# A decoder layer on one core: operand splits around the end of the latents, two products alternating, a longer last stretch by rows

## The chip, the cores and the metric

The kernel runs on one core of one Trainium2 chip, whose other cores have nothing to do. The metric is the time of one execution on the device in microseconds (us); lower is better. The kernel before takes 638.35 us, the median of 3 runs (637.8 to 639.55).

## What is computed

The layer has an attention, a second product with a context after quantization, and a feed-forward part with a routed branch, each followed by a residual and a normalization. The change lies in the feed-forward part alone, on `[2, 512, 1024]` tokens:

```python
logits = jnp.einsum('bsh,he->bse', hidden_states, gate_w)
routing_weights, selected_experts = jax.lax.top_k(logits, K)
h = jax.nn.relu(jnp.einsum('bsh,hi->bsi', hidden_states, up_w)) ** 2
shared_out = jnp.einsum('bsi,ih->bsh', h, down_w)
x_latent = jnp.einsum('bsh,hl->bsl', hidden_states, fc1_w)
expert_out = jnp.einsum('bsl,lm->bsm', x_latent, expert_w)
moe_out = expert_out * jnp.sum(routing_weights, axis=-1, keepdims=True)
routed_out = jnp.einsum('bsl,lh->bsh', moe_out, fc2_w)
return _layernorm(shared_out + routed_out, ln_gamma, ln_beta)
...
x = _layernorm(x + _L0_ffn_ref(x, ...), axis=-1)
```

K is 2, INT (hidden) 2048, LAT 512. Everything is float32 of full precision, so every product on TensorE is three: each operand is split into a high part (what the array's format holds) and a low part (the rest), and hi·hi, hi·lo and lo·hi are added in PSUM (`split_products`).

## The kernel before, in words

`decoder` runs `attention_and_cross` (the first 209 us) and then, behind a barrier of all engines, `feed_forward`. That is written by hand: one program for each engine, in the order in which its instructions stand, held together by semaphores. `then_inc` on an instruction counts its semaphore up, and `wait_ge` holds all that stands behind it on that engine.

**Products up.** `MU` = 20 blocks m of 128 hidden or latent rows, 8 contraction tiles k each, for batches 0 and 1: `product(m, b)` is 24 matmuls of 128x512 (8 tiles, three products) into one of four PSUM banks `acc_b`. The stationary operand is the weight block, whose parts `u_hi` (ScalarE) and `u_lo` (VectorE) are made by a `split_u(m)` on each of the two; the moving operand is the token matrix, transposed. Batch 0's is there when the feed-forward begins, and so are the products (0, 0) and (1, 0). Batch 1's is made at the beginning: `transpose_x1(k)` is four transposes of TensorE into a bank of `acc_a`, `x1T_hi_out(k)` on ScalarE copies it, `x1T_lo_out(k)` on VectorE subtracts, and `product(0, 1)` takes tile k as it comes, with `transpose_x1(k + 2)` behind it (two banks). Then come four small transposes of the routing logits (`transpose_logits(0)`), and `product(1, 1)`. On VectorE, `route(0)` stands behind the eight `x1T_lo_out`: it reads the transposed logits, and turns them into the routing weights; behind it stand `split_u(2)` and `split_u(3)`. GpSimd adds beta to the rows of the residual meanwhile (`add_beta`, L2030). Blocks 16 to 19 of the up products are the latents: VectorE multiplies them by the routing weights (`latent(m, b)`).

**Products down.** The second matrix product is done by a scheme with seven products instead of eight (`PHASES`, in the order p1, p7, p6, p4, p5, p2, p3). Each phase has NP = 10 contraction tiles k for BT = 4 row tiles t; a step (k, t) is three matmuls of 128x512, a pair of k's (`j`) is 24. The left operand of a pair is split into `oa` (three slots, `oa_hi_out` on ScalarE, the low part by `lo_out` on VectorE); the right one into `ob` (`ob_hi_out`, and `lo_out` again), except in p2 and p3, where it lies split in DRAM and is loaded by GpSimd's queue (`load_split`, 1 MB a pair, once the slot's last reader is done). Each phase fills four PSUM banks, `acc_a` and `acc_b` in turn. On VectorE the last thing before the phases is `latent(19, 1)`, which waits for the very last up product; `lo_out("p1", 0)` stands behind it.

**The end.** p3 runs k outermost for its first tiles, and for its last `TAIL` = 6 tiles row by row, so that rows t = 0 to 3 are complete one after the other. For each, VectorE adds (`p3_out`), takes statistics, centres, scales and adds the residual (`half_stats`, `centre`, `add_x2`); ScalarE squares and takes roots (`first_root`, `last_root`) and normalizes (`final_norm`); SyncE's queue stores the row tile, 512 KB.

Of the kernel before, what the change touches and what calls it, by code (L numbers as in the profile page):

```python
# [17 lines left out]
F32 = mybir.dt.float32  # L18
# [1244 lines left out]
NX = 4  # L1263
TAIL = 6
PHASES = ("p1", "p7", "p6", "p4", "p5", "p2", "p3")
# [13 lines left out]
def step(phase, j):  # L1279
    return PHASES.index(phase) * PAIRS + j  # L1280


def feed_forward(nc, so, args, x2_dram, w2_dram, t_dram, r_dram, x2b_dram, out):
# [8 lines left out]
    with ExitStack() as ctx:  # L1292
# [8 lines left out]
        xT_hi, xT_lo = [so["x2T_hi"], x1_hi], [so["x2T_lo"], x1_lo]  # L1301
        f1b0, f2b0, f1b1 = [sb(n, [P, NP, SEQ], F32) for n in ("f1b0", "f2b0", "f1b1")]
# [10 lines left out]
        pairs_of = lambda x, i: x[:, 4 * i:4 * i + 4].rearrange("p (s h) c -> p s h c", h=2)  # L1313
        oa = [pairs_of(x, i) for x, i in ((xT_hi[0], 0), (xT_hi[0], 1), (xT_lo[0], 0))]
        ob = [pairs_of(x, i) for x, i in ((xT_lo[0], 1), (x1_hi, 0), (x1_hi, 1), (d_op, 0), (d_op, 1))]
# [20 lines left out]
        stage_hi, stage_lo = [[x[h][:, KH // 2:NP] for x in stage] for h in range(2)]  # L1336
        acc_b, acc_a = [so["psum"][:, i:i + BT] for i in (0, BT)]
        acc_of = lambda phase: (acc_a, acc_b)[PHASES.index(phase) % 2]

# [11 lines left out]
            b_hi_done b_lo_done eps_done beta_done st_done mv_done rootA_done rsA_done gam_done res_done nmean_done square_done  # L1351
            rootB_done rsB_done nb_done out_done""".split()
        S = {**so["sem"], **{n: sem("f_" + n) for n in names}}
# [14 lines left out]

        order = [b * BT + t for b in (1, 0) for t in range(BT)]
        half_of = lambda b, t, n: ffn[b * BT + t][:, n * BANK:(n + 1) * BANK]  # L1370
        up_products = BATCH * 2 * UP
# [21 lines left out]
        def a_raw(phase, j):  # L1393
            return s3_of(j) if phase == "p7" else pair({"p1": f1b0, "p6": f1b0, "p5": f1b1, "p4": f2b1, "p3": f1b0, "p2": f2b0}[phase], j)

        def ob_slot(s):
# [23 lines left out]
        def _(sp):  # L1420
# [69 lines left out]
            for n in range(BT, TILES):  # L1490
                load_x2(n)
            for n in range(TILES):
                i = order[n]
                sp.wait_ge(S["out_done"], n + 1)
                sp.dma_start(out_rows[i * P:(i + 1) * P, :], ffn[i]).then_inc(out_st, 16)
            sp.wait_ge(out_st, 16 * TILES)

        @block.tensor
        def _(pe):
            def transpose_x1(k):  # L1500

                if k >= 2:
                    pe.wait_ge(S["x1T_lo_done"], k - 1)
                for t in range(BT):
                    mm = pe.transpose(acc_a[:, k % 2, t * P:(t + 1) * P], x2_tok[:, t, k * P:(k + 1) * P], ident[:])  # L1505
                mm.then_inc(S["x1T_ready"], 1)
# [19 lines left out]
            def spread_r(b):  # L1526
# [5 lines left out]
                mm.then_inc(S["rT_ready"], 1)  # L1532

            def product(m, b):

                q = product_index(m, b)
                if q >= 4 and q - 4 < up_products:
                    pe.wait_ge(S["relu_done"], q - 3)
                elif q >= 4:
                    pe.wait_ge(S["lat_done"], q - 4 - up_products + 1)  # L1540
                pe.wait_ge(S["u_lo_done"], m + 1)
                for k in range(KT):
                    if b and m == 0:
                        pe.wait_ge(S["x1T_lo_done"], k + 1)
                    st = [u[:, m % 2, k] for u in (u_hi, u_lo)]
                    for i, (s, v) in enumerate(split_products(st, (xT_hi[b][:, k], xT_lo[b][:, k]))):
                        mm = pe.matmul(acc_b[:, q % 4], s, v, start=(k == 0 and i == 0), stop=(k == KT - 1 and i == 2))  # L1547
                    if (m, b) == (0, 1) and k + 2 < KT:
                        transpose_x1(k + 2)
                mm.then_inc(S["op_used"], 1)  # L1550

            def tile_step(phase, k, t):
# [18 lines left out]
                if t == 0 and k % 2 == 0:  # L1571
# [3 lines left out]
                    else:  # L1575
                        pe.wait_ge(ob_in[ob_slot(s)], 16 * ((s - PARKED) // PAIRS + 1))
                st = [oa[s % RD][:, k % 2, i, t * P:(t + 1) * P] for i in range(2)]
                for i, (a, v) in enumerate(split_products(st, [ob[ob_slot(s)][:, k % 2, i] for i in range(2)])):
# [34 lines left out]
        def _(act):  # L1613
            def x1T_hi_out(k):
                act.wait_ge(S["x1T_ready"], k + 1)
                act.activation(x1_hi[:, k], acc_a[:, k % 2], ACT.Copy).then_inc(S["x1T_hi_done"], 1)  # L1616

# [30 lines left out]
            def oa_hi_out(phase, j):  # L1648
                s = step(phase, j)
                if s >= RD:  # L1650
                    consumed(act, s - RD)
                else:
                    act.wait_ge(S["op_used"], product_index(MU - 1, 0) + 1)
                a_ready(act, phase, j)
                act.activation(oa[s % RD][:, :, 0], a_raw(phase, j), ACT.Copy).then_inc(S["oa_hi_done"], 1)  # L1655

# [28 lines left out]
            def final_norm(n):  # L1685
                i = order[n]
                act.wait_ge(S["nb_done"], n + 1)
                act.activation(ffn[i], ffn[i], ACT.Identity, bias=nbias[:, n:n + 1], scale=rstd[:, 1, n:n + 1]).then_inc(S["out_done"], 1)

# [54 lines left out]
            first_root(1)  # L1744
            oa_hi_out("p3", 0)
            final_norm(0)
            last_root(1)
            first_root(2)
            oa_hi_out("p3", 1)
            final_norm(1)  # L1750
            last_root(2)
            first_root(3)
            oa_hi_out("p3", 2)
            final_norm(2)
            last_root(3)
            oa_hi_out("p3", 3)
            final_norm(3)
            oa_hi_out("p3", 4)
            first_root(BT)
            for n in range(BT, TILES):  # L1760
                last_root(n)
                if n + 1 < TILES:
                    first_root(n + 1)
                final_norm(n)

        @block.vector
        def _(dve):
            def x1T_lo_out(k):
                dve.wait_ge(S["x1T_hi_done"], k + 1)
                dve.tensor_tensor(x1_lo[:, k], acc_a[:, k % 2], x1_hi[:, k].bitcast(F32), ALU.subtract).then_inc(S["x1T_lo_done"], 1)  # L1770

# [74 lines left out]
            def lo_out(phase, j):  # L1846
                s = step(phase, j)
                dve.wait_ge(S["oa_hi_done"], s + 1)
                dve.tensor_tensor(oa[s % RD][:, :, 1], a_raw(phase, j), oa[s % RD][:, :, 0].bitcast(F32), ALU.subtract).then_inc(S["oa_lo_done"], 1)
# [145 lines left out]
            last_bias(0)  # L1995
            add_x2(1)
            centre(2, 2 * BT)
            lo_out("p3", 0)
            last_bias(1)
            add_x2(2)  # L2000
            centre(3, 2 * BT)
            lo_out("p3", 1)
            last_bias(2)
            add_x2(3)
            lo_out("p3", 2)
            p2_out()
            last_bias(3)
            lo_out("p3", 3)
            for n in range(BT, TILES):
                half_stats(n, 0)  # L2010
            lo_out("p3", 4)
            for t in range(BT):
# [6 lines left out]
                add_x2(n)  # L2019
            last_bias(TILES - 1)  # L2020

        @block.gpsimd
# [118 lines left out]
```

## Time and profile before

| | |
|---|---|
| median of 3 runs | 638.35 us (637.8 to 639.55) |
| the profiled execution | 643.53 us, its span 641.7 us |
| outside the span | 1.83 us |
| mean granted clock of TensorE | 0.979 |
| busy: TensorE, VectorE, ScalarE, GpSimd | 93%, 59%, 47%, 19% of the span |
| chain that ended last | TensorE 62%, VectorE 4%, ScalarE 1% |
| largest lines of it | L1547 (up products) 32%, L1579 (phases) 28% |

The span is from the first to the last instruction. The chain is followed back from the last instruction, at each step to what released it. Times in the rows below are from the span's start. The granted clock is 1.00 at 2.4 GHz and 0.50 at 1.2 GHz.

### The profile page before, as it was taken

How to read it: one execution, taken by the hardware profiler on the slowest of the kernel's cores; microseconds unless marked ns; L12 is line 12 of the kernel's file. 1: busy time of each engine (PE TensorE's matmuls, PEld its weight loads, DVE VectorE, ACT ScalarE, POOL GpSimd, SP SyncE). 2: the span in 40 equal slices, each digit the busy share in tenths (PEclk: the TensorE clock that was granted, in tenths of full speed). 3: DMA queues.
4: the chain of work that ended last, by engine and by line, in shares of the span. 5: the costliest groups of instructions: out<-in, count | busy, mean ns of one | idle time of the engine just before them, and what ended most of it. 6: DMA issues, size and time to landing. Idle time of an engine off the chain costs nothing.

```text
span 641.7 us, 9374 instructions
## 1 busy us (share of the span) xinstructions
PE 597.9 (93%) x3718; PEld 480.2 (75%) x3728; DVE 379.6 (59%) x514; ACT 299.4 (47%) x384; POOL 121.3 (19%) x162
## 2 busy tenths in 40 slices
PE   2799999898999799999999999998999999999991
PEld 1687877566776588788888888877888888888881
DVE  4937898889663373335333331419764565749875
ACT  4456687896693534333333331022344333314625
POOL 2811254635441042222110000000000000021000
PEclk9899999999999899999999999997999999999997
DMA  9766675583663868699799664003333336089903
GB/s 335 273 175 179 189 198 157 156 271 100 192 199 131 295 215 309 219 332 361 231 362 307 253 229 164 0 1 107 94 97 97 98 99 230 1 281 323 279 36 131
DMA packets 82108, 123.61 MB, mean 193 GB/s; under 512 B 23824, under 2 KB 50704, under 8 KB 82064
## 3 DMA queue, kind: packets, MB, share of 16 engines
q1 hardware_dynamic: 74592, 95.21, 44.4%
q0 software_dynamic: 5168, 19.40, 9.6%
q10 hardware_dynamic: 2304, 8.39, 4.0%
q8 instruction: 30, 0.49, 0.3%
q14 instruction: 14, 0.11, 0.1%
HBM read 83.13 MB, written 35.65 MB: 185 GB/s over the span
## 4 chain that ended last, share of the span: by engine, by line
PE 62%; DVE 4%; ACT 1%; issue 0%; DVEq 0%; ACTq 0%
PE psum L1547 32%; PE psum L1579 28%; PE psum L1505 0%; DVE stat_n L1901 0%; DVE x1T_lo L1770 0%; DVE ffn_lo L1920 0%; DVE ffn_hi L1920 0%; DVE ffn_hi L1909 0%; DVE ffn_lo L1909 0%; ACT x1T_hi L1616 0%; PE psum L1513 0%; PE psum L1514 0%; PE psum L1531 0%; DVE ffn_hi L1894 0%; ACT hx L1679 0%
## 5 line engine op out<-in xcount | busy, mean ns | idle before, releaser
L1774 DVE TENSOR_TENSOR u_lo<-u_raw,u_hi 128x1024 fp32r<-128x1024 f32 x18 | 23.8, 1320 | 84.3 <-ACT u_hi L1621 84.3
L1547 PE MATMUL psum<-x1T_hi,u_hi 128*128 128x512 f32 x160 | 63.4, 396 | 2.4 <-DVE x1T_lo L1770 2.4
L1547 PE MATMUL psum<-x1T_hi,u_lo 128*128 128x512 f32 x160 | 62.8, 392 | 0.0
L1547 PE MATMUL psum<-x1T_lo,u_hi 128*128 128x512 f32 x160 | 62.7, 392 | 0.0
L1579 PE MATMUL psum<-x2T_lo,x2T_hi 128*128 128x512 f32 x240 | 58.9, 403 | 3.1 <-DVE x2T_lo L1852 3.1
L1579 PE MATMUL psum<-x1T_hi,x2T_hi 128*128 128x512 f32 x264 | 61.5, 389 | 0.0
L1579 PEld LDWEIGHTS psum<-x1T_hi,x2T_hi 128*128 128x128 f32 x264 | 49.6, 188 | 10.3
L1579 PEld LDWEIGHTS psum<-x2T_lo,x2T_hi 128*128 128x128 f32 x240 | 47.0, 196 | 13.6 <-issue 3.5
L1547 PE MATMUL psum<-x2T_hi,u_hi 128*128 128x512 f32 x144 | 56.3, 391 | 0.0
L1547 PE MATMUL psum<-x2T_lo,u_hi 128*128 128x512 f32 x144 | 56.1, 389 | 0.0
L1547 PE MATMUL psum<-x2T_hi,u_lo 128*128 128x512 f32 x144 | 56.0, 389 | 0.0
L2046 POOL DMA_DIRECT2D x1T_hi<-r_scratch x4 | 2.8, 711 | 251.8 <-PE psum L1579 251.8
L1579 PE MATMUL psum<-x1T_hi,x2T_lo 128*128 128x512 f32 x216 | 50.4, 389 | 0.0
L341 PE MATMUL psum<-w_hi,xT_hi 128*128 128x512 f32 (+1 forms) x128 | 35.9, 363 | 13.7 <-POOL w_lo L1132 8.2
L1579 PEld LDWEIGHTS psum<-x1T_hi,x2T_lo 128*128 128x128 f32 x216 | 40.6, 188 | 8.4
L1655 ACT ACTIVATE x2T_hi<-f1b 128x1024 fp32r<-128x1024 f32 x14 | 14.8, 1060 | 53.3 <-PE psum L1579 38.1
L1547 PEld LDWEIGHTS psum<-x1T_hi,u_hi 128*128 128x128 f32 x160 | 30.2, 189 | 9.5 <-DVE x1T_lo L1770 2.2
L1547 PEld LDWEIGHTS psum<-x1T_hi,u_lo 128*128 128x128 f32 x160 | 30.3, 189 | 6.2
L1547 PEld LDWEIGHTS psum<-x1T_lo,u_hi 128*128 128x128 f32 x160 | 30.2, 189 | 5.9
L341 PE MATMUL psum<-w_lo,xT_hi 128*128 128x512 f32 (+1 forms) x128 | 34.5, 352 | 0.0
L341 PEld LDWEIGHTS psum<-w_hi,xT_hi 128*128 128x128 f32 x128 | 20.5, 196 | 18.6 <-issue 8.8
L341 PE MATMUL psum<-w_hi,xT_lo 128*128 128x512 f32 (+1 forms) x128 | 34.2, 349 | 0.0
(255 smaller groups left out, 1220.2 us busy)
## 6 DMA issues: line engine op xcount, KB each, us to landing
d_raw<-in_L_ffn_down_w_dram SPq DMA_DIRECT2D x20, 512.0 KB, 7.2
t_scratch<-d_raw SPq DMA_DIRECT2D x20, 512.0 KB, 5.8
d_raw<-t_scratch SPq DMA_DIRECT2D x20, 512.0 KB, 3.8
c_sb<-in_ctx_dram ACTq DMA_DIRECT2D x16, 512.0 KB, 3.6
u_raw<-in_L_ffn_up_w_dram SPq DMA_DIRECT2D x16, 512.0 KB, 5.2
r_scratch<-f1b SPq DMA_DIRECT2D x10, 512.0 KB, 5.3
r_scratch<-f2b SPq DMA_DIRECT2D x10, 512.0 KB, 4.6
x_sb<-in_x_dram SPq DMA_DIRECT2D x8, 512.0 KB, 5.2
```

Of the source, the lines that this page charges most:

```text
L341: mm = pe.matmul(qkv_ps[:, c0:c1], s, v, start=(k == 0 and i == 0), stop=(k == KT - 1 and i == 2))
L1547: mm = pe.matmul(acc_b[:, q % 4], s, v, start=(k == 0 and i == 0), stop=(k == KT - 1 and i == 2))
L1579: mm = pe.matmul(acc_of(phase)[:, t], a, v, start=(k == 0 and i == 0), stop=(k == NP - 1 and i == 2))
L1655: act.activation(oa[s % RD][:, :, 0], a_raw(phase, j), ACT.Copy).then_inc(S["oa_hi_done"], 1)
L1774: dve.tensor_tensor(u_lo[:, m % 2], u_raw[:, m % 2], u_hi[:, m % 2].bitcast(F32), ALU.subtract).then_inc(S["u_lo_done"], 1)
L2046: pool.dma_start(ob[ob_slot(s)].rearrange("p s h c -> p s (h c)"), r_dram[k * P:(k + 2) * P, n].rearrange("(s p) h c -> p s (h c)", p=P)). ...
```

## The change

Four edits, all in `feed_forward`:

1. **Batch 1 of blocks 0 and 1.** `first_products` takes the place of `product(0, 1)`, `transpose_logits(0)`, `product(1, 1)`. Three banks of `acc_a` (0, 1 and 3) hold transposed tiles, so three groups of transposes stand at the head. For k = 0 to 2 tile k of block 0 is followed by tile k of block 1; block 1's tiles 3 to 7 stand behind all of block 0's. `transpose_logits(0)`, which uses bank 3, stands behind both.
2. **Low parts between the last latents.** On VectorE `lo_out("p1", 0)` stands between `latent(19, 0)` and `latent(19, 1)`.
3. **`TAIL` = 8.** p3's left operand gets two more slots (`oa_last`, in the memory of `f2b0`, free once p2's operand is split), and pairs 0 and 1 of p3 are written without waiting for p2's pairs to be used; `lo_out("p3", ...)`, `oa_hi_out("p3", ...)`, `last_bias(3)` and `p2_out()` change places with it.
4. **The last row tile.** VectorE normalizes its first 512 columns and ScalarE the others; SyncE's queue stores the one half and ScalarE's queue the other.

```diff
-TAIL = 6
+TAIL = 8
...
+        x1T_bank = lambda k: acc_a[:, (0, 1, 3)[k % 3]]
...
+        def oa_slot(s):
+
+            first = step("p3", 0)
+            if s < first:
+                return s % RD
+            return RD + s - first if s < first + 2 else s - first - 2
...
-            for n in range(TILES):
+            for n in range(TILES - 1):
                 i = order[n]
                 sp.wait_ge(S["out_done"], n + 1)
                 sp.dma_start(out_rows[i * P:(i + 1) * P, :], ffn[i]).then_inc(out_st, 16)
-            sp.wait_ge(out_st, 16 * TILES)
+            sp.wait_ge(S["half_done"], 1)
+            sp.dma_start(last_rows[:, 0:BANK], ffn[order[-1]][:, 0:BANK]).then_inc(out_st, 16)
+            sp.wait_ge(out_st, 16 * (TILES + 1))
...
             def transpose_x1(k):
 
-                if k >= 2:
-                    pe.wait_ge(S["x1T_lo_done"], k - 1)
+                if k >= 3:
+                    pe.wait_ge(S["x1T_lo_done"], k - 2)
...
+            def first_products():
+
+                for k in range(3):
+                    transpose_x1(k)
+                pe.wait_ge(S["u_lo_done"], 2)
+                for k in range(KT):
+                    pe.wait_ge(S["x1T_lo_done"], k + 1)
+                    mm = contraction(0, 1, k)
+                    if k < 3:
+                        contraction(1, 1, k)
+                    if k + 3 < KT:
+                        transpose_x1(k + 3)
+                mm.then_inc(S["op_used"], 1)
+                for k in range(3, KT):
+                    mm = contraction(1, 1, k)
+                mm.then_inc(S["op_used"], 1)
...
-            transpose_x1(0)
-            transpose_x1(1)
-            product(0, 1)
+            first_products()
             transpose_logits(0)
-            product(1, 1)
...
             def oa_hi_out(phase, j):
                 s = step(phase, j)
-                if s >= RD:
+                if s >= step("p3", 2):
+                    consumed(act, s - PAIRS)
+                elif s >= step("p3", 0):
+                    act.wait_ge(S["s4_done"], PAIRS)
+                    act.wait_ge(S["oa_hi_done"], s)
+                    act.wait_ge(S["oa_lo_done"], step("p2", PAIRS - 1) + 1)
+                elif s >= RD:
                     consumed(act, s - RD)
...
+            act.wait_ge(S["out_done"], TILES)
+            act.dma_start(last_rows[:, BANK:EMB], ffn[order[-1]][:, BANK:EMB]).then_inc(out_st, 16)
...
                 if m >= 2 * UP:
-                    for b in range(BATCH):
-                        latent(m, b)
+                    latent(m, 0)
+                    if m == MU - 1:
+                        lo_out("p1", 0)
+                    latent(m, 1)
...
-            for j in range(PAIRS):
+            for j in range(1, PAIRS):
                 lo_out("p1", j)
...
-            lo_out("p3", 2)
+            lo_out("p3", 3)
+            last_bias(3)
             p2_out()
-            last_bias(3)
-            lo_out("p3", 3)
+            lo_out("p3", 4)
             for n in range(BT, TILES):
                 half_stats(n, 0)
-            lo_out("p3", 4)
...
             last_bias(TILES - 1)
+            dve.wait_ge(S["nb_done"], TILES)
+            dve.tensor_scalar(ffn[order[-1]][:, 0:BANK], ffn[order[-1]][:, 0:BANK], rstd[:, 1, TILES - 1:TILES], nbias[:, TILES - 1:TILES],
+                              ALU.mult, ALU.add).then_inc(S["half_done"], 1)
```

In the rows of the program below a semaphore's number that was used in the first part goes by that part's name (`wraw_in6` is `oa_lo_done`).

TensorE where batch 1 of blocks 0 and 1 ends, before (f2b are the rows being transposed, hx at L1522 the logits):

```order
L1547 MATMUL psum<-x1T_hi,u_hi 128x512 [waits f_x1T_lo_done]
L1547 MATMUL psum<-x1T_lo,u_hi 128x512
L1547 MATMUL psum<-x1T_hi,u_lo 128x512
L1522 MATMUL psum<-ident,hx 128x16 [waits f_lgT_done]
L1522 MATMUL psum<-ident,hx 128x16 x3
L1547 MATMUL psum<-x1T_hi,u_hi 128x512 [waits u_lo_done]
```

and now, from the last tiles of block 1 on:

```order
L1552 MATMUL psum<-x1T_hi,u_hi 128x512
L1552 MATMUL psum<-x1T_lo,u_hi 128x512
L1552 MATMUL psum<-x1T_hi,u_lo 128x512
L1536 MATMUL psum<-ident,hx 128x16 [waits f_lgT_done]
L1536 MATMUL psum<-ident,hx 128x16 x3
L1552 MATMUL psum<-x2T_hi,u_hi 128x512 [waits u_lo_done,f_relu_done]
```

The logits' transposes stood between the two products, with block 1's 24 matmuls behind them; now both products stand ahead of them, and right behind them stands `product(2, 0)`, which waits for the low part of `u` (`u_lo_done`).

VectorE at the last latents, before (f2b<-psum is `latent`; x2T_hi is the left operand's slot, x2T_lo the right one's):

```order
L1780 TENSOR_TENSOR f1b<-psum,hx 128x512 [waits f_rT_done,op_used] x2
L1780 TENSOR_TENSOR f2b<-psum,hx 128x512 [waits f_rT_done,op_used] x2
L1849 TENSOR_TENSOR x2T_hi<-f1b,x2T_hi 128x2x512 [waits bias_in]
L1852 TENSOR_TENSOR x2T_lo<-d_raw,x2T_lo 128x2x512 [waits wraw_in7]
L1849 TENSOR_TENSOR x2T_hi<-f1b,x2T_hi 128x2x512 [waits bias_in]
```

and now:

```order
L1819 TENSOR_TENSOR f1b<-psum,hx 128x512 [waits f_rT_done,op_used] x2
L1819 TENSOR_TENSOR f2b<-psum,hx 128x512 [waits f_rT_done,op_used]
L1888 TENSOR_TENSOR x2T_hi<-f1b,x2T_hi 128x2x512 [waits bias_in]
L1891 TENSOR_TENSOR x2T_lo<-d_raw,x2T_lo 128x2x512 [waits wraw_in7]
L1819 TENSOR_TENSOR f2b<-psum,hx 128x512 [waits f_rT_done,op_used]
L1888 TENSOR_TENSOR x2T_hi<-f1b,x2T_hi 128x2x512 [waits bias_in]
```

The two subtractions of p1's pair 0 moved up past the last latent.

TensorE in p3, from its third pair on, before:

```order
L1579 MATMUL psum<-x1T_hi,x2T_hi 128x512 [waits ob_in2,wraw_in6]
L1579 MATMUL psum<-x1T_hi,x2T_hi 128x512 x23
L1579 MATMUL psum<-x2T_lo 128x512 [waits ob_in0,wraw_in6]
L1579 MATMUL psum<-x2T_lo 128x512 x5
L1579 MATMUL psum<-d_op,x2T_hi 128x512 [waits ob_in3,wraw_in6]
L1579 MATMUL psum<-d_op,x2T_hi 128x512 x5
L1579 MATMUL psum<-d_op,x2T_hi 128x512 [waits ob_in4,wraw_in6]
L1579 MATMUL psum<-d_op,x2T_hi 128x512 x5
```

and now, from its second pair on:

```order
L1611 MATMUL psum<-x1T_hi,oa_last 128x512 [waits ob_in2,wraw_in6]
L1611 MATMUL psum<-x1T_hi,oa_last 128x512 x5
L1611 MATMUL psum<-x2T_lo,x2T_hi 128x512 [waits ob_in0,wraw_in6]
L1611 MATMUL psum<-x2T_lo,x2T_hi 128x512 x5
L1611 MATMUL psum<-d_op,x2T_hi 128x512 [waits ob_in3,wraw_in6]
L1611 MATMUL psum<-d_op,x2T_hi 128x512 x5
L1611 MATMUL psum<-d_op,x2T_lo 128x512 [waits ob_in4,wraw_in6]
L1611 MATMUL psum<-d_op,x2T_lo 128x512 x5
```

Each wait for a loaded right-hand pair (`ob_in`) stood 24 or, in the first row of the last stretch, 6 matmuls behind the one before; now four of them, not three, are 6 matmuls apart.

## Rows read from the trace of the kernel before

**Rows 1.** Waits of TensorE: us in all, times, longest us

```profile
PE psum L1579 <- DVE x2T_lo L1852: 3.1, 1, 3.1
PE psum L1547 <- DVE x1T_lo L1770: 2.4, 4, 1.2
```

**Rows 2.** Chain of waits, front of the feed-forward: start, us, what

```profile
218.59 0.45 PE psum L1505 x4
219.06 0.61 ACT x1T_hi L1616
219.69 0.70 DVE x1T_lo L1770
...
224.22 0.35 PE psum L1522 x4
```

**Rows 3.** Chain of waits, 300 to 440 us: the unbroken products

```profile
301.62 130.59 PE psum L1547 x576
```

**Rows 4.** Windows: granted clock is the third number from the end

```profile
212.10:215.90 3.80, 3.80 (x13) 3.07 (x14) 1.14 (x2) 1.16 (x3) 0.00 (x0) 0.55 1.13 334
215.90:220.00 4.10, 3.82 (x24) 2.95 (x22) 1.69 (x3) 3.14 (x6) 0.56 (x1) 1.00 1.01 407
435.30:441.10 5.80, 5.77 (x14) 4.55 (x15) 5.76 (x6) 0.00 (x0) 0.00 (x0) 0.50 0.58 181
441.10:445.00 3.90, 3.90 (x19) 3.19 (x18) 3.46 (x4) 1.17 (x2) 0.00 (x0) 0.99 0.37 120
```

**Rows 5.** Timeline, 224 to 230 us, VectorE and GpSimd

```profile
224.61 0.19 DVE L1786 COPY lg<-psum 128x32 f32<-128x32 f32 x1 [1.40 <-PE psum L1522]
224.82 2.39 POOL L2030 TENSOR_TENSOR s_own<-s_own,hx 128x1024 f32<-128x1024 f32 x1 [5.58 <-DMA s_own<-x_scratch]
225.46 1.98 DVE L1795 TENSOR_TENSOR r_tok<-top 128x1 f32<-128x1 f32 x4
228.27 1.22 DVE L1774 TENSOR_TENSOR u_lo<-u_raw,u_hi 128x1024 fp32r<-128x1024 f32 x1
```

**Rows 6.** Line L1795: duration ns min/median/max

```profile
L1795 DVE TENSOR_TENSOR r_tok<-top x8: 147/152/1774, 225.5 to 294.3; 128x1 f32<-128x1 f32 x8
```

**Rows 7.** Timeline, 427 to 435 us, ScalarE and VectorE

```profile
427.75 1.04 ACT L1662 ACTIVATE x2T_lo<-d_raw 128x1024 fp32r<-128x1024 f32 x1
...
432.23 1.06 ACT L1662 ACTIVATE x1T_hi<-d_raw 128x1024 fp32r<-128x1024 f32 x1 [2.48 <-PE psum L1547]
432.23 0.69 DVE L1780 TENSOR_TENSOR f2b<-psum,hx 128x512 f32<-128x512 f32 x1 [4.75 <-PE psum L1547]
432.84 1.22 DVE L1849 TENSOR_TENSOR x2T_hi<-f1b,x2T_hi 128x1024 fp32r<-128x1024 f32 x1
433.97 1.22 DVE L1852 TENSOR_TENSOR x2T_lo<-d_raw,x2T_lo 128x1024 fp32r<-128x1024 f32 x1
```

**Rows 8.** Timeline, tail, TensorE, then VectorE, then ScalarE

```profile
625.90 2.88 PE L1579 MATMUL psum<-d_op,x2T_hi 128*128 128x512 f32 x12
...
613.56 1.23 DVE L1849 TENSOR_TENSOR x2T_hi<-f1b,x2T_hi 128x1024 fp32r<-128x1024 f32 x1 [1.83 <-ACT x2T_hi L1655]
616.58 0.69 DVE L1894 TENSOR_TENSOR ffn_hi<-psum,ffn_hi 128x512 f32<-128x512 f32 x1 [1.79 <-PE psum L1579]
...
630.57 0.68 DVE L1894 TENSOR_TENSOR ffn_lo<-psum,ffn_lo 128x512 f32<-128x512 f32 x1
...
637.43 1.24 ACT L1688 ACTIVATE ffn_lo<-ffn_lo,nbias,rstd_f 128x1024 f32<-128x1024 f32 x1 [0.43 <-DVE nbias L1929]
```

**Rows 9.** Line L1616: an activation of half the width

```profile
L1616 ACT ACTIVATE x1T_hi<-psum x8: 592/597/600, 210.6 to 221.9; 128x512 fp32r<-128x512 f32 x8
```

**Rows 10.** Tile d_op, 595 us on: loads of the last right-hand pairs

```profile
L2046 POOL DMA_DIRECT2D d_op<-r_scratch x2: 696/702/707, 596.4 to 601.9; - x2
DMA to landing us min/median/max: 7.7/7.8/7.9
```

**Rows 11.** DMA, 630 us on: KB each, median us to landing

```profile
out_dram<-ffn_lo SPq DMA_DIRECT2D x2, 512.0 KB, 2.6
```

More of the change, by code:

```diff
@@ L1301, in feed_forward @@
         xT_hi, xT_lo = [so["x2T_hi"], x1_hi], [so["x2T_lo"], x1_lo]
-        f1b0, f2b0, f1b1 = [sb(n, [P, NP, SEQ], F32) for n in ("f1b0", "f2b0", "f1b1")]
+        f1b0, f1b1 = [sb(n, [P, NP, SEQ], F32) for n in ("f1b0", "f1b1")]
+        with nc.sbuf_tensor("oa_last", [P, 8, SEQ], F32R) as oa_last:
+            pass
+        f2b0 = sb("f2b0", [P, NP, SEQ], F32)
         f2b1 = so["f2b1"]
@@ L1313, in feed_forward @@
         pairs_of = lambda x, i: x[:, 4 * i:4 * i + 4].rearrange("p (s h) c -> p s h c", h=2)
-        oa = [pairs_of(x, i) for x, i in ((xT_hi[0], 0), (xT_hi[0], 1), (xT_lo[0], 0))]
+        oa = [pairs_of(x, i) for x, i in ((xT_hi[0], 0), (xT_hi[0], 1), (xT_lo[0], 0), (oa_last, 0), (oa_last, 1))]
         ob = [pairs_of(x, i) for x, i in ((xT_lo[0], 1), (x1_hi, 0), (x1_hi, 1), (d_op, 0), (d_op, 1))]
@@ L1351, in feed_forward @@
             b_hi_done b_lo_done eps_done beta_done st_done mv_done rootA_done rsA_done gam_done res_done nmean_done square_done
-            rootB_done rsB_done nb_done out_done""".split()
+            rootB_done rsB_done nb_done out_done half_done""".split()
         S = {**so["sem"], **{n: sem("f_" + n) for n in names}}
@@ L1369, in feed_forward @@
         order = [b * BT + t for b in (1, 0) for t in range(BT)]
+        last_rows = out_rows[order[-1] * P:(order[-1] + 1) * P, :]
         half_of = lambda b, t, n: ffn[b * BT + t][:, n * BANK:(n + 1) * BANK]
@@ L1532, in spread_r, with contraction @@
                 mm.then_inc(S["rT_ready"], 1)
+            def contraction(m, b, k):
+                st = [u[:, m % 2, k] for u in (u_hi, u_lo)]
+                for i, (s, v) in enumerate(split_products(st, (xT_hi[b][:, k], xT_lo[b][:, k]))):
+                    mm = pe.matmul(acc_b[:, product_index(m, b) % 4], s, v, start=(k == 0 and i == 0), stop=(k == KT - 1 and i == 2))
+                return mm
+            def first_products():
[13 more added lines that the diff above has]
+                mm.then_inc(S["op_used"], 1)
             def product(m, b):
@@ L1542, in product @@
                 for k in range(KT):
[L1543 to L1549, printed above, removed]
+                    mm = contraction(m, b, k)
                 mm.then_inc(S["op_used"], 1)
@@ L1576, in tile_step @@
                         pe.wait_ge(ob_in[ob_slot(s)], 16 * ((s - PARKED) // PAIRS + 1))
-                st = [oa[s % RD][:, k % 2, i, t * P:(t + 1) * P] for i in range(2)]
+                st = [oa[oa_slot(s)][:, k % 2, i, t * P:(t + 1) * P] for i in range(2)]
                 for i, (a, v) in enumerate(split_products(st, [ob[ob_slot(s)][:, k % 2, i] for i in range(2)])):
@@ L1615, in x1T_hi_out @@
                 act.wait_ge(S["x1T_ready"], k + 1)
-                act.activation(x1_hi[:, k], acc_a[:, k % 2], ACT.Copy).then_inc(S["x1T_hi_done"], 1)
+                act.activation(x1_hi[:, k], x1T_bank(k), ACT.Copy).then_inc(S["x1T_hi_done"], 1)
             def split_u(m):
@@ L1654, in oa_hi_out @@
                 a_ready(act, phase, j)
-                act.activation(oa[s % RD][:, :, 0], a_raw(phase, j), ACT.Copy).then_inc(S["oa_hi_done"], 1)
+                act.activation(oa[oa_slot(s)][:, :, 0], a_raw(phase, j), ACT.Copy).then_inc(S["oa_hi_done"], 1)
             def ob_hi_out(phase, j):
@@ L1687, in final_norm @@
                 act.wait_ge(S["nb_done"], n + 1)
-                act.activation(ffn[i], ffn[i], ACT.Identity, bias=nbias[:, n:n + 1], scale=rstd[:, 1, n:n + 1]).then_inc(S["out_done"], 1)
+                cols = slice(BANK if n == TILES - 1 else 0, EMB)
+                act.activation(ffn[i][:, cols], ffn[i][:, cols], ACT.Identity, bias=nbias[:, n:n + 1],
+                               scale=rstd[:, 1, n:n + 1]).then_inc(S["out_done"], 1)
             w2_stored(act)
@@ L1745, in _ @@
             oa_hi_out("p3", 0)
+            oa_hi_out("p3", 1)
             final_norm(0)
@@ L1748, in _ @@
             first_root(2)
-            oa_hi_out("p3", 1)
+            oa_hi_out("p3", 2)
             final_norm(1)
@@ L1848, in lo_out @@
                 dve.wait_ge(S["oa_hi_done"], s + 1)
-                dve.tensor_tensor(oa[s % RD][:, :, 1], a_raw(phase, j), oa[s % RD][:, :, 0].bitcast(F32), ALU.subtract).then_inc(S["oa_lo_done"], 1)
+                dve.tensor_tensor(oa[oa_slot(s)][:, :, 1], a_raw(phase, j), oa[oa_slot(s)][:, :, 0].bitcast(F32), ALU.subtract).then_inc(S["oa_lo_done"], 1)
                 if s < PARKED:
@@ L1996, in _ @@
             add_x2(1)
+            lo_out("p3", 0)
             centre(2, 2 * BT)
-            lo_out("p3", 0)
+            lo_out("p3", 1)
             last_bias(1)
```

11 lines of the change are left out of this document (5 added, 6 removed).

## Prediction

> **What bounds the kernel now.** I read the waits of TensorE first, then the chain of waits, then the granted clock by windows, then the timelines of the places that the change touches. The reader is to see that in the feed-forward TensorE alone sets the pace. From 301.62 us it runs 576 matmuls in 130.59 us without a break [rows 3]: 0.227 us each, 0.68 for a contraction tile of three, 5.44 for 24. A gap on TensorE there lengthens the kernel by its own length, and so does half a clock. There are two gaps. The first is at the front, where batch 1 is transposed: 2.4 us in four waits for `x1T_lo` [rows 1]. The second is between the last latent and the first phase: 3.1 us in one wait [rows 1]. After each the clock is low: a mean of 0.55 from 212.1 to 215.9 and 0.50 from 435.3 to 441.1, and full behind that [rows 4]. Only in the tail is the bound another one: TensorE ends at 628.78, and VectorE begins its last row tile at 630.57 [rows 8].
>
> All sums are against the profiled execution (643.53 us, span 641.7), which took 5.2 us or 0.8% more than the median of the runs, 638.35. I carry the differences over to the median unchanged.
>
> **Edit 1, the front: what it gives.** From 215.9 (full clock again, [rows 4]) to the logits' transposes at 224.22 [rows 2] 8.3 us pass. TensorE's own work there is six tiles of `product(0, 1)`, 6 x 0.68 = 4.1, and four groups of transposes at 0.45 [rows 2], 1.8: in all 5.9. So it idles for 2.4 us, in the loop of transposes 0.45, ScalarE 0.61, VectorE 0.70 [rows 2]. Tiles 0 to 2 of block 1 and a third bank fill these holes; the third group of transposes moves into the wait at the head, 0.4 more. Stepping the new order through with these durations I find no wait left that is longer than 0.2 us. The same 48 products thus end some 2.8 us earlier, and 0.35 more because the logits' transposes [rows 2] are no longer in between. Before they end at 224.57 + 5.44 = 230.0; now at 226.9, and with 0.1 for the waits at 227.0.
>
> **Edit 1: what it takes.** Before, the logits' transposes were followed by 5.44 us of `product(1, 1)`. Under that cover VectorE did `route(0)` and then the low part of u for block 2, which `product(2, 0)` waits for: from the transposes' begin at 224.22 [rows 2] to 228.27 + 1.22 = 229.49 [rows 5] are 5.27 us. It was ready just 0.5 us before it was wanted. Now the transposes stand behind both products, and the cover is gone. The chain is 5.27 us long, with one thing to take off: of the eight additions at L1795 seven take about 0.15 us and one takes 1.77 [rows 6]; it stands in the four of 1.98 us that ended as GpSimd's addition of 224.82 + 2.39 = 227.21 did [rows 5]. The new `route(0)` reads its logits at about 227.4, behind that addition, so I take 1.6 off. 227.0 + 5.27 - 1.6 + 0.1 (from the release to the matmul) gives 230.8 for the first matmul of `product(2, 0)`, against 230.0 before: **+0.8 us**. ScalarE's part of u is made long before, since block 0 ends earlier, and the other users of `acc_b` have what they wait for.
>
> With this TensorE stands idle from 227.3 to 230.8, 3.5 us, longer than the gap of 3.1 behind which the clock stayed at 0.50 for 5.8 us [rows 1, 4]. No row shows this stall, so its clock is bounded by the two that are there: 5.8 x 0.5 = 2.9 us lost behind the second gap, 3.8 x 0.45 = 1.7 behind the first; at best nothing. I take the mean of the two, **+2.3**. The front: +3.1, between +0.8 and +3.7, and 1.6 more if VectorE is held up again. The low clock at 212.1 itself stays: the idle stretch ahead of it is only a little shorter.
>
> **Edit 2, the junction.** Before, TensorE ends the products at 432.21 [rows 3], VectorE multiplies the last latent at 432.23, and only then makes the two low parts, at 432.84 and 433.97, done at 435.19 [rows 7]. Their high parts were ready at 428.8 [rows 7]. Moved ahead of that latent, the two subtractions fill 427.9 to 430.2 on an engine that idled there, and TensorE goes on at 432.2. The wait of 3.1 [rows 1] goes, and with it the 5.8 us at half clock, 2.9 [rows 4]: **-6.0 us**. The clock's part may be as small as the front's 1.7, so -4.8 to -6.0. What is late next? Pair 1: its right high part waits for the very last product and is done at 433.3, and VectorE's subtraction behind it at 435.2 [rows 7], as before. TensorE wants it at 432.2 + 5.44 = 437.6: 2.4 us to spare. Behind it VectorE has two subtractions of 1.22 and one or two sums of the same length for each pair, at most 4.9 of 5.44 us.
>
> **Edit 3, the rows of the tail.** With six tiles a row takes TensorE 18 x 0.227 = 4.1 us; VectorE's begin at 616.58 and 630.57 [rows 8], 4.66 apart. It falls behind, and starts the last row 1.79 us after TensorE's end. With eight tiles a row takes 5.44, VectorE keeps up, and starts the last one 0.04 behind TensorE: **-1.75**. For that all five left operands must be there at 611 instead of 615. The last was split at 613.56 because it waited for a slot [rows 8]; with the new slots it is released at 601.5, at p2's end, and in VectorE's new order I step it to 607.6. The new order also puts one subtraction of p3 ahead of some normalizing of batch 1, which has slack. The right-hand pairs are the tight ones. The last is issued at 601.9 and lands after 7.9 us [rows 10], at 609.8. It was wanted 24 + 3 x 6 matmuls behind p3's second pair, and now 3 x 6: at 601.5 + 5.44 + 4.1 = 611.0. That leaves 1.2 us; cost nothing, at worst 1.3 (below).
>
> **Edit 4, the last tile.** ScalarE's 1.24 us [rows 8] becomes an activation of half the width, 0.60 [rows 9]; VectorE's half runs beside it. **-0.65.** The store lands 2.6 us after its issue [rows 11]; two halves on two queues carry the same bytes, so I count it as equal, within 0.4 either way, since the trace shows no such pair.
>
> **Sum.** +3.1 - 6.0 - 1.75 - 0.65 = -5.3 us. The profiled execution would be 638.2, the median **633.1 us**, 0.8% less.
>
> **A rule about VectorE's wait.** By the rows, one addition of one column took 1.77 us beside GpSimd's [rows 5, 6]. The Trainium skill ("SBUF — State Buffer", "Who interferes with whom") says that a VectorE instruction with two SBUF inputs contends with a GpSimd instruction that reads SBUF; by that rule the trace agrees, and the additions are slow again wherever they meet one.
>
> **A rule about the clock.** The two low stretches lasted 3.8 and 5.8 us [rows 4]. The Trainium skill ("TensorE: Matmul & The Clock Gate", Part 1) says that the half clock is the default which activity releases, and that the point of the change differs from run to run; of the same kernel, then, either gap may cost either amount.
>
> **The rivals.**
> - *The front's stall is too short for the clock.* A pause that is cut by 0.3 us of small transposes near its start leaves it up. For it: the waits between 215.9 and 220, well under 1 us each, left it at 1.00 [rows 4]. Against it: 3.5 us is more than the 3.1 that sufficed. -7.6, 630.8 us.
> - *The additions meet GpSimd again.* It decides whether the load ahead of GpSimd's addition lands 0.3 us later or the products end 0.3 us sooner. +1.6: 634.7 us. The skill's rule above is this rival.
> - *The front's holes stay,* since ScalarE has relu and square between its copies. Then the products end 2 us later: 635.1 us. Against it: the three tiles of block 1 are 2 us of work that needs nothing new.
> - *The last right-hand pair is late.* A store of 512 KB, earlier now with its normalizing, falls into its flight and takes part of the bandwidth. 512 KB at the rate of this load (1 MB in 7.9 less some 2) is up to 2.5 us; that less 1.2 is 1.3 of idle TensorE: 634.4 us.
> - *The junction's gap moves by a pair,* the other side. Place: p1's pair 1; point: its low part is later than 437.6, which takes 2.4 us more on VectorE. Full price at 5.5 more: all 6.0 are lost, and -5.3 becomes +0.7, 639.1 us, with the front's stall as the net effect. Against it: nothing on VectorE ahead of it is new.
>
> **How the numbers follow.** The forecast has 0.60, the clock that stays up 0.10, the second collision 0.10, the late pair 0.10, the holes that stay 0.06, the gap that moves 0.04. The forecast itself reaches from 631.5 (clock cheap in front) to 635 (clock cheap at the junction, slow stores). The range 630.5 to 636.2 leaves out the last rival and the ends of the others. 0.3% is 1.9 us, about what a measurement of this kernel can tell from none: faster than 636.4 has 0.89, between that and 640.3 are most of the last rival and sums of two bad ones, 0.08; slower 0.03.
>
> **What would show it.** Right: a wait of about 3.5 us of TensorE for `u_lo` near 230 with 0.50 behind it; none at 432 and a clock of 1.00 through it; the same matmuls from there to the end 6 us sooner; VectorE's last row within 0.1 us of TensorE's end; the last activation at 0.6. Wrong: no wait for `u_lo`, or one longer than 4 us; a wait for p1's second pair, or for the last pair in p3.

## The result, and the profile after

The changed kernel takes 637.13 us (median of 15 runs, 634.49 to 639.77) against 639.15 us (median of 15 runs, 635.82 to 642.95): ratio 0.9961, 95% interval 0.9942 to 0.9980. By the ratio that is 2.5 us faster (1.3 to 3.7), where 5.3 were forecast, and 637.13 lies above the range's upper end of 636.2. The sign and the places were right, the size was less than half.

The profiled execution after has a span of 637.1 us, 4.6 shorter than before's 641.7. What it shows of the three places, first the waits of TensorE (us in all, times, longest):

```profile
PE psum L1552 <- DVE u_lo L1813: 4.6, 1, 4.6
PE psum L1552 <- DVE x1T_lo L1809: 0.7, 1, 0.7
```

The wait of 3.1 us for `x2T_lo` at the first phase [rows 1] is gone, the waits for `x1T_lo` are down from 2.4 to 0.7, and a new one of 4.6 us for the low part of u stands in their place. The chain of waits at the front (start, us, what):

```profile
211.40 0.64 PE psum L1519 x4
...
221.59 1.39 PE psum L1552 x6
...
223.01 4.36 PE psum L1552 x18
227.37 0.36 PE psum L1536 x4
227.75 0.20 DVE lg L1825
...
228.61 1.52 DVE r_tok L1834 x4
...
231.02 1.14 DVE u_lo L1813
...
232.30 3.88 PE psum L1552 x9
```

Behind the products (they end at 227.37) stand the logits' transposes, the whole route and u's low part on VectorE, and only then `product(2, 0)` at 232.30. From the first transposes (211.40) that is 20.9 us; before it was 230.0 - 209.9 = 20.1. The granted clock (third number from the end) of the stretches that answer to [rows 4]:

```profile
212.10:215.90 3.80, 3.08 (x20) 2.53 (x19) 1.98 (x3) 2.68 (x6) 0.80 (x1) 1.00 0.83 233
232.30:235.70 3.40, 3.40 (x8) 2.63 (x9) 3.37 (x5) 0.00 (x0) 0.54 (x1) 0.52 0.68 198
430.70:436.10 5.40, 5.40 (x25) 4.47 (x25) 3.05 (x3) 2.96 (x3) 0.00 (x0) 1.00 0.15 26
436.10:445.00 8.90, 8.90 (x41) 7.38 (x40) 8.76 (x9) 4.97 (x5) 0.00 (x0) 1.00 0.34 104
```

The half clock is where the new stall is, and nowhere else in this part: not at 212, where the one profile of before had it, and not at the first phase. There TensorE goes on without a break; the chain from 300 us on:

```profile
305.56 130.57 PE psum L1552 x576
436.14 190.41 PE psum L1611 x840
...
626.58 0.70 DVE ffn_lo L1933
```

840 matmuls in 190.41 us are 0.2267 each; before, the first 786 of them took 181.2 us, 3.0 more than at that pace:

```profile
435.33 181.22 PE psum L1579 x786
```

The tail, VectorE, then ScalarE and its queue, and the last two stores (KB, us to landing):

```profile
604.67 1.22 DVE L1888 TENSOR_TENSOR x2T_lo<-f1b,x2T_lo 128x1024 fp32r<-128x1024 f32 x1
...
610.26 0.69 DVE L1933 TENSOR_TENSOR ffn_hi<-psum,ffn_hi 128x512 f32<-128x512 f32 x1 [1.99 <-PE psum L1611]
...
626.58 0.69 DVE L1933 TENSOR_TENSOR ffn_lo<-psum,ffn_lo 128x512 f32<-128x512 f32 x1 [0.60 <-PE psum L1611]
...
633.44 0.55 DVE L2063 TENSOR_SCALAR ffn_lo<-ffn_lo,rstd_f,nbias 128x512 f32<-128x512 f32 x1
...
633.44 0.81 ACT L1724 ACTIVATE ffn_lo<-ffn_lo,nbias,rstd_f 128x512 f32<-128x512 f32 x1 [0.42 <-DVE nbias L1968]
634.28 0.35 ACTq L1803 DMA_DIRECT2D out_dram<-ffn_lo  x1
```

```profile
out_dram<-ffn_lo SPq DMA_DIRECT2D x1, 256.0 KB, 2.0
out_dram<-ffn_lo ACTq DMA_DIRECT2D x1, 256.0 KB, 2.5
```

The last left operand is split at 604.67 (before at 613.56, [rows 8]), each row finds VectorE waiting (the first for 1.99 us), and the last one starts at 626.58, 0.03 us behind TensorE's end; before it was 1.79 late. From TensorE's end to the span's end are 10.6 us, before 12.9.

Counted inside these two profiles the feed-forward is 6.1 us shorter (425.7 from the first transposes to the end, before 431.8), more than was forecast. The runs say 2.5. The mechanisms are all there. The question is what the edits cost and give in most runs, and what the one profile of before showed larger than it usually is.

### The profile page after: what moved, and what is told of

It reads as the page before. It is cut to its first block, busy times and chain, and to the rows that moved or that the text cites. A ratio compares the mean times of both kernels' runs of the same rounds, so it can differ in the third digit from the quotient of the medians.

```text
span 637.1 us, 9378 instructions
## 1 busy us (share of the span) xinstructions
PE 595.8 (94%) x3718; PEld 479.8 (75%) x3728; DVE 378.5 (59%) x515; ACT 299.5 (47%) x384; POOL 123.0 (19%) x162
## 4 chain that ended last, share of the span: by engine, by line
PE 64%; DVE 2%; ACT 0%; issue 0%; DVEq 0%; ACTq 0%
PE psum L1552 33%; PE psum L1611 30%; PE psum L1519 0%; PE psum L1527 0%; PE psum L1528 0%; PE psum L1545 0%; DVE r_tok L1834 0%; DVE ffn_lo L1959 0%; DVE ffn_lo L1948 0%; ACT hx L1714 0%; DVE u_lo L1813 0%; ACT ffn_lo L1724 0%; DVE hx L1839 0%; PE psum L1536 0%; DVE stat_n L1940 0%
## 5 line engine op out<-in xcount | busy, mean ns | idle before, releaser
L1813 DVE TENSOR_TENSOR u_lo<-u_raw,u_hi 128x1024 fp32r<-128x1024 f32 x18 | 25.5, 1420 | 85.2 <-ACT u_hi L1650 85.2
L1611 PE MATMUL psum<-x2T_lo,x2T_hi 128*128 128x512 f32 x264 | 62.1, 389 | 0.0
L1611 PEld LDWEIGHTS psum<-x2T_lo,x2T_hi 128*128 128x128 f32 x264 | 49.6, 188 | 10.3
L1611 PE MATMUL psum<-x1T_hi,x2T_hi 128*128 128x512 f32 x216 | 50.4, 389 | 0.0
L1611 PEld LDWEIGHTS psum<-x1T_hi,x2T_hi 128*128 128x128 f32 x216 | 40.6, 188 | 8.4
L1552 PEld LDWEIGHTS psum<-x2T_hi,u_hi 128*128 128x128 f32 x144 | 27.4, 190 | 10.5 <-issue 4.7
```

The lines of the kernel that those rows point to most:

```text
L1552: mm = pe.matmul(acc_b[:, product_index(m, b) % 4], s, v, start=(k == 0 and i == 0), stop=(k == KT - 1 and i == 2))
L1611: mm = pe.matmul(acc_of(phase)[:, t], a, v, start=(k == 0 and i == 0), stop=(k == NP - 1 and i == 2))
L1813: dve.tensor_tensor(u_lo[:, m % 2], u_raw[:, m % 2], u_hi[:, m % 2].bitcast(F32), ALU.subtract).then_inc(S["u_lo_done"], 1)
```

## The experiments

**The three parts alone.** `front_only` is the kernel before with edit 1, `junction_only` with edit 2, `tail_only` with edits 3 and 4; their diffs are the parts of the diff above. `junction_only`, for one:

```diff
-                    for b in range(BATCH):
-                        latent(m, b)
+                    latent(m, 0)
+                    if m == MU - 1:
+                        lo_out("p1", 0)
+                    latent(m, 1)
...
-            for j in range(PAIRS):
+            for j in range(1, PAIRS):
                 lo_out("p1", j)
```

> The kernel before with edit 1 alone (both products of batch 1 ahead of the logits' transposes). Theory A (each edit does what the profiles show, and only how long the half clock lasts differs from run to run): the wait for u_lo stands near 230 us, 3.5 to 4.6 us long, with half a clock behind it; 2 to 4 us slower than before. Rival B (the front is fairly free and the gain of the other edits is what is missing): within 1 us of before. Rival C (the front costs much more than in the one profile, since GpSimd's addition usually meets the route's): 5 us or more slower.

> The kernel before with edit 2 alone (p1's first low parts ahead of the last latent). Theory A: the gap of 3.1 us goes in every run, the half clock behind it cost between 0 and 2.9, by chance; 3.1 to 5 us faster than before, not the 6.0 of the forecast. Rival B: the gap only moves, or is made up later; under 2 us faster, with a wait in p1 or p7.

> The kernel before with edits 3 and 4 alone (TAIL 8, the last tile in halves). Theory A: 2.4 us faster, VectorE's last row within 0.1 us of TensorE's end. Rival B: 1 us or less, since a load of p3 is late in some runs or the two stores cost more.

| | ratio to before (95%) | us | forecast |
|---|---|---|---|
| front alone | 1.0094 (1.0064 to 1.0125) | +6.0 | +3.1 |
| junction alone | 0.9921 (0.9896 to 0.9947) | -5.0 | -6.0 |
| tail alone | 0.9954 (0.9927 to 0.9981) | -2.9 | -2.4 |
| sum | | -1.9 | -5.3 |
| the change | 0.9961 (0.9942 to 0.9980) | -2.5 | |

(us: the ratio times 639.) The parts add up to the change within their intervals. The junction's gain is at the upper end of theory A's 3.1 to 5 us, the tail's is a little over the forecast, and the front costs about twice what was forecast (4.1 to 8.0 us by its interval): more than theory A's 2 to 4, and where rival C put it. Rival C's reason, the meeting with GpSimd's addition, is only part of it, as the runs below show. Waits and granted clock of `front_only`:

```profile
PE psum L1539 <- DVE u_lo L1790: 4.7, 1, 4.7
PE psum L1598 <- DVE x2T_lo L1868: 3.1, 1, 3.1
```

```profile
232.60:239.10 6.50, 6.42 (x16) 5.05 (x17) 4.79 (x6) 0.00 (x0) 0.54 (x1) 0.52 0.80 213
439.90:447.20 7.30, 6.25 (x15) 4.95 (x16) 7.27 (x7) 0.90 (x1) 0.00 (x0) 0.53 0.49 145
```

The new wait is 4.7 us, and this time the half clock lasts 6.5 us behind it, where the profile of the changed kernel has 3.4. The old gap at the junction, still there in this kernel, has 7.3 us of it. In `tail_only`, with the same old gap of 3.1 us, it is 3.4 us:

```profile
210.00:214.00 4.00, 3.60 (x20) 2.87 (x21) 1.95 (x3) 2.39 (x5) 0.00 (x0) 1.00 1.12 327
433.00:436.40 3.40, 3.40 (x10) 2.63 (x9) 3.37 (x3) 0.00 (x0) 0.00 (x0) 0.51 0.62 204
```

The matmuls behind the junction say what that costs. Their chain in `junction_only`, where there is no gap, in `front_only` and in `tail_only`:

```profile
431.55 178.19 PE psum L1579 x786
```

```profile
440.95 181.31 PE psum L1598 x786
```

```profile
431.98 192.30 PE psum L1593 x840
```

In `front_only` the half clock took 3.1 us, in `tail_only` 1.9 (840 matmuls take 190.4 at full clock), behind the same gap. And the front's low clock of before (212.1 to 215.9, [rows 4]) is in none of the other profiles with the old front (`tail_only`, `junction_only` and, below, `no_front` and `fill_junction`).

**The clock's part, alone.** Work that nobody needs is put into either gap, so that TensorE waits as long as before but isn't idle. `fill_front` on the changed kernel, and `fill_junction` on the kernel before:

```diff
             first_products()
             transpose_logits(0)
+            for i in range(16):
+                pe.matmul(acc_a[:, 0], xT_hi[0][:, 0, 0:P], xT_hi[0][:, 1], start=True, stop=True)
```

```diff
+            for i in range(3):
+                pe.matmul(acc_a[:, 0], ident[:], f2b0[:, 0], start=True, stop=True)
             for phase in PHASES[:-1]:
```

> The changed kernel with 16 products of 128x512 on batch 0's tokens, into a bank that nobody reads, behind the logits' transposes: TensorE works for 3.6 of the 4.6 us in which it waits for u_lo. It takes the clock's part alone out of the front's stall. Theory A (the stall costs its own length and then half a clock for 3.4 or 6.8 us, 1.7 or 3.4 us lost): the wait shrinks to about 1 us with product(2, 0) at the same place, the clock stays at 1.00, and the kernel is 1.7 to 3 us faster than the changed one. Rival B (the clock isn't what makes the front dearer than forecast): within 1 us of the changed kernel.

> The kernel before with three products in full float32 (the identity by a hidden block, 128x512, four passes each, about 2.6 us) into a bank that nobody reads, between the last up product and p1, where TensorE waits 3.1 us. It takes the clock's part alone out of the junction. Theory A (the half clock behind the gap costs 0 to 3.4 us by chance): the first phase starts at the same place with the clock at 1.00; 1.3 to 2 us faster than before, which with the gap's own 3.1 makes the 4.5 to 5 us of the junction alone. Rival B (the forecast's 2.9 is what the clock costs in every run): 2.9 us or more faster.

`fill_front`: ratio to before 0.9907 (0.9877 to 0.9938), 5.9 us faster than before and 3.4 faster than the changed kernel. `fill_junction`: 0.9978 (0.9956 to 1.0001), 1.4 us. Chain and windows of `fill_front`, then the chain of `fill_junction`:

```profile
224.11 0.36 PE psum L1536 x4
...
229.55 11.16 PE psum L1552 x48
```

```profile
227.90:231.00 3.10, 1.88 (x8) 1.24 (x8) 3.10 (x5) 0.00 (x0) 0.46 (x2) 1.00 0.47 182
229.50:240.00 10.50, 10.45 (x46) 8.68 (x47) 4.76 (x6) 1.23 (x2) 0.73 (x2) 1.00 0.85 286
```

```profile
301.56 130.59 PE psum L1547 x576
435.28 178.42 PE psum L1579 x786
```

`product(2, 0)` starts 5.4 us behind the begin of the logits' transposes, 0.5 later than in the changed kernel (the route's additions take 2.0 us here instead of 1.5), and the clock stays at 1.00. The same at the junction: p1 starts 3.1 us late as ever, but 786 matmuls take 178.4 us instead of 181.2. At the junction the half clock thus costs 1.4 us a run (2.8 to nothing), not 2.9: rival B of `fill_junction` is just outside the interval. With the gap's own 3.1 this gives 4.5 for edit 2, and 5.0 was measured (3.4 to 6.6).

In the front the times give 3.4 us for the clock, with some 2.3 either way, since two measured ratios are subtracted. The profiles have less in them: from `product(2, 0)` to the begin of the unbroken products 73.3 us pass in the changed kernel and 74.6 in `front_only`, against 71.7 in `fill_front`, so the clock took 1.6 and 2.9. A second measure is the time lost to the clock in each run, its span times one less its mean granted clock (idle stretches are counted in it): on average 8.0 us in the changed kernel and 5.5 with the filler, 9.0 before and 7.0 with the junction filled. That is 2.5 and 2.0 us, with some 1.8 and 1.3 either way. The clock's part is shown in both places; its size in the front is known only as 2 to 3 us or a little more.

**The route's additions.** `add_beta_later` is the changed kernel with GpSimd's additions held back:

```diff
+            pool.wait_ge(S["u_lo_done"], 4)
             for n in range(TILES):
                 add_beta(n)
```

> The changed kernel with GpSimd's first addition of beta held until the low part of u for block 3 is done. Theory A (one of the route's small additions waits for GpSimd's): the four take 0.4 instead of 1.5 us, the wait for u_lo is 3.4 to 3.6 instead of 4.6 us, 1.1 us faster than the changed kernel. Rival B (they are slow for another reason): 1.5 us as before, no gain.

First the changed kernel, then this one:

```profile
227.54 2.34 POOL L2074 TENSOR_TENSOR s_own<-s_own,hx 128x1024 f32<-128x1024 f32 x1 [7.01 <-DMA s_own<-x_scratch]
...
228.61 1.51 DVE L1834 TENSOR_TENSOR r_tok<-top 128x1 f32<-128x1 f32 x4
```

```profile
225.07 0.37 DVE L1834 TENSOR_TENSOR r_tok<-top 128x1 f32<-128x1 f32 x4
```

```profile
PE psum L1552 <- DVE u_lo L1813: 3.5, 1, 3.5
```

The four additions take 0.37 us when GpSimd is quiet and 1.51 when its addition (227.54 to 229.88) lies over them; the wait for u_lo falls from 4.6 to 3.5. Theory A holds to 0.1 us. Timed, the kernel has 0.9921 (0.9891 to 0.9950), 2.5 us faster than the changed one; 1.1 was expected, and the interval of 1.9 us either way takes it in. The half clock still stands behind the shorter stall in its profile (0.58 over the first 4.1 us). That the additions meet GpSimd's again was a rival of the prediction, and it is what happened in the changed kernel, in `front_only` (1.58 us) and in `fill_front` (2.01). The forecast had the route begin 0.2 us behind that addition; but the load ahead of it lands 7.6 us after its issue (219.98 to 227.54), before 6.1, and the addition comes 1.2 us later against the first transposes. Over the profiles (but `add_beta_later`, where the addition is held back) this load took 6.1 to 6.8 us with the old front and 7.2 to 8.0 with the new one; why was not tried.

**Taking the stall away.** Three ways: `u_before_route` and `logits_between` on the changed kernel, and `no_front`, the changed kernel without edit 1. The first swaps two calls behind `transpose_logits(0)`:

```diff
-            route(0)
             split_u(2)
+            route(0)
             split_u(3)
```

The second puts the logits' transposes inside the alternating products:

```diff
                 mm.then_inc(S["op_used"], 1)
+                transpose_logits(0)
                 for k in range(3, KT):
                     mm = contraction(1, 1, k)
                 mm.then_inc(S["op_used"], 1)
...
             first_products()
-            transpose_logits(0)
```

> The changed kernel with one line moved on VectorE: the low part of u for block 2 ahead of route(0), behind the transposed tiles. Theory A: the wait of 4.6 us for u_lo and the half clock behind it (1.7 us) go, nothing else changes: product(2, 0) follows the logits' transposes at once; 5 to 7 us faster than the changed kernel, 8 to 9 faster than before. Rival B (the front's stall isn't what holds the change back): within 2 us of the changed kernel.

> The changed kernel with the logits' transposes right behind block 0's last tile, ahead of the last five tiles of block 1. Theory A: 3.4 us of products lie over the route again, the wait for u_lo is 1 to 1.6 us, too short to lower the clock; 5 us faster than the changed kernel (3.4 of the wait and 1.7 or more of the clock), 7 faster than before. Rival B (order on TensorE matters little): within 2 us of the changed kernel.

> The changed kernel without edit 1 (its front as before; junction and tail changed). Theory A (the edits add up): 7 to 8 us faster than before, 5 to 6 faster than the changed kernel; the front is all that the change loses by. Rival B (the gains of junction and tail overlap): 5 us or less faster than before.

`u_before_route`: 0.9858 (0.9816 to 0.9900), 9.1 us faster than before. `logits_between`: 0.9867 (0.9830 to 0.9904), 8.5. `no_front`: 0.9901 (0.9863 to 0.9938), 6.3. The chain of `u_before_route`:

```profile
209.42 0.64 PE psum L1519 x4
...
225.44 0.35 PE psum L1536 x4
225.78 6.36 PE psum L1552 x27
```

`product(2, 0)` follows the logits' transposes at once, 16.4 us behind the first ones: 4.5 less than in the changed kernel, and 2.1 less than with the old front at full clock (18.5 in `tail_only`). One line moved makes the change's gain over three times as large (9.1 against 2.5). In `logits_between` no wait for u_lo was left at all, where 1 to 1.6 us were expected: the route, begun 3.4 us sooner against the first transposes, has its additions done (0.37 us) before GpSimd's begins. `no_front` is 3.8 us faster than the changed kernel, 5 to 6 were expected; its 6.3 (4.0 to 8.8) lies between theory A and rival B and excludes neither, and the two parts measured alone add up to 7.9.

`front_u_first` is the kernel before with edit 1 and that one line, and `both_orders` the changed kernel with both edits of this section:

> The kernel before with edit 1 and with the low part of u for block 2 made ahead of route(0), junction and tail as before. Theory A: what edit 1 gives by itself, from the first transposes to product(2, 0) 16.4 us where the kernel before takes 18.5 at full clock; 2.1 us faster than before, 8 us faster than edit 1 alone. Rival B (the alternation itself gives nothing, only the stall costs): within 0.5 us of before.

> The changed kernel with both: u's low part ahead of route(0), and the logits' transposes between block 0's last tile and block 1's last five. Theory A (with u ahead nobody waits for the route any more): the same as with u ahead alone, 9 us faster than before, within 1 us of that kernel. Rival B (the route's place still matters): over 1 us faster than with u ahead alone.

`front_u_first`: 0.9959 (0.9934 to 0.9984), 2.6 us faster, theory A's 2.1 within its interval. Alternating the products is worth what it was made for; 8.6 us lie between this kernel and edit 1 alone, for the order of two calls on VectorE. `both_orders`: 0.9840 (0.9810 to 0.9869), 10.2 us faster than before and 1.1 less than `u_before_route`, which their intervals (about 2 us each) don't separate. The profiles say that the second edit adds nothing: from the first transposes to the end are 419.5 us here, 419.6 in `u_before_route` and 419.6 in `logits_between`. Its front:

```profile
207.16 0.64 PE psum L1519 x4
...
219.75 0.34 PE psum L1536 x4
220.09 14.51 PE psum L1552 x63
```

It has the lowest ratio of all kernels run, and by these spans `u_before_route` and `logits_between` are as good.

## Why the prediction was right in its places and wrong in its size

- **The bound, and the new stall.** "The cover is gone" held to the letter: a wait for u_lo near 230 us, with 0.50 behind it. This was the one term with a plus sign, and it was the term most mis-sized: +3.1 forecast, +6.0 measured (4.1 to 8.0), from the two parts that follow. The wait of 4.6 us was also over the 4 us that the prediction itself had named as a sign of being wrong.
- **Its own length, "+0.8 us": 2.4.** From the first transposes to `product(2, 0)` are 20.9 us, against 18.5 in the kernels with the old front at full clock. Two things make the 1.6 between 0.8 and 2.4. First, the additions met GpSimd's: from the logits' transposes to `product(2, 0)` are 4.9 us instead of the 3.8 of the sum. It was priced at 1.6 as a rival with 0.10; it should have been the case itself, since the margin was 0.2 us. Second, I stepped the new order through with the low clock of 212 to 216 in it. At full clock TensorE reaches the transposed tiles sooner and waits for them again (0.7 us at the last one), and the products end 16.0 us behind the first transposes, not 15.4, which is the forecast's 17.1 less the 1.7 of that clock. Between the two profiles the difference is the forecast's +0.8 (20.1 to 20.9), but by luck: the prediction said that the low clock at 212 stays, and it was gone, which made up for the 1.6.
- **Its clock, "the mean of the two, +2.3".** The timed filler gives 3.4 us, with 2.3 either way, and the profiles 1.6 and 2.9, so these runs don't show the 2.3 wrong by itself. With 2.4 of the front's own length it makes 4.0 to 5.8 of the 6.0 measured. Both neighbours in the trace stood behind shorter pauses, and one profile gives one draw.
- **The junction, "-6.0 us": -5.0.** The gap of 3.1 and the half clock's 5.8 us went as told. But 2.9 us of clock was one execution's; filled with idle work the gap gives 1.4 a run. This was in the text as a bound (-4.8); the sum still took the dear end here and the mean in front. The Trainium skill ("TensorE: Matmul & The Clock Gate", Part 1), which the prediction named for it, says that the point of the change differs from run to run. The traces agree: behind this one gap the half clock lasted 3.4 us in `tail_only` and 7.3 in `front_only`.
- **"I carry the differences over to the median unchanged."** This is the step that failed for the whole, and it had no reason beside it. Against its own profile the forecast came near (6.1 us shorter from the first transposes on, where 5.3 were forecast), helped by that low clock; against the runs it did not. The profiled execution had a low stretch at 212, which no other profile of the old front has, and the long one behind the junction (1.7 and some 3.0 us lost). It lay 4.4 us above the later median of 639.15. By its mean granted clock of 0.979 it had lost 13.5 us of its span to the clock, where the 70 runs of the same kernel that were timed beside the experiments lost 8.9 on average, so nearly all of the excess is the clock's. What it had lost by chance could not be won in the median.
- **The tail, "-1.75" and "-0.65".** In the two profiles 2.3 us, of the same two parts: VectorE's lag is gone, 1.76; ScalarE's half took 0.81 us instead of 0.60, so 0.43. [Rows 9] was a plain copy, the last operation has scale and bias as columns. At full width the rows had the same 0.2 between the two, 1.04 to 1.06 [rows 7] against 1.24 [rows 8]; that the columns cause it was not tried by itself. The right-hand pair was no trouble: it landed 7.6 to 8.1 us after its issue, and TensorE didn't wait. The price of that rival was itself added up too low: 512 KB at 1 MB in 5.9 us is 2.95 us, not 2.5, so 1.8 us of idle TensorE and not 1.3.
- **The range.** It was built around a likeliest case with one chance outcome at its favourable end. With the terms as now measured (2.4 and 1.6 to 3.4 in front, 3.1 and 1.4 at the junction, 2.3 to 2.9 in the tail) the sum is -1.0 to -3.4, and the measured -2.5 (1.3 to 3.7 faster) lies in it; the terms are no better known than to 1 or 2 us. The base was a draw too: the three first runs had a median of 638.35, fifteen have 639.15, so 0.8 of the distance to the forecast of 633.1 is the base's.

## What to carry to other kernels

When work is pulled forward on the bound engine, ask what the moved piece covered: what stood under it on another engine, and who waits for the last instruction there. A small step that nobody needs soon (here the route) shouldn't stand ahead of one that the bound engine needs next. And a profile in which the clock fell is one draw: price a gap by its own length, and the clock by several executions, or by filling the gap with idle work.

## What the runs showed of the hardware

The same kernel's runs differ mostly by the clock. Of the changed kernel's 15, the three with a mean granted clock of 0.993 took 634.5 us each, and the two with 0.983 took 638.9 and 639.4. The low stretches behind the two gaps came in two lengths, some 3.4 us (1.7 to 1.9 lost in matmuls) and 5.8 to 7.3 (2.9 to 3.1 lost), also behind the same gap. Part of the difference lies outside the change: in the attention part, the same code in all kernels, the profile of the changed kernel has a stretch at 0.66 between 150 and 155 us that the one of before lacks, and over the 13 profiles the feed-forward's first transposes stand anywhere from 206.5 to 211.7 us. In the one profile of each filled kernel the clock stayed up: with 16 matmuls (3.9 us) in a stretch of 5.1, and with 2.7 us of them in one of 3.1.

The four additions of one column took 0.37 us on VectorE by themselves and 1.5 to 2.6 beside GpSimd's addition of 128x1024.
